# A transformer block on one core: projections and transposes placed anew over the even steps, the second layer norm moved up, the bias sum behind the rounding

## What is computed

```python
x = x + attn(layernorm(x))          # x: 16 x 512 x 256
x = x + ffn(layernorm(x))
# attn: qkv = x @ qkv_w.T + qkv_b; softmax(q k^T / 4) v; then @ proj_w.T + proj_b
# ffn:  clip(x / input_scale, -448, 448) rounded to float8_e4m3fn, times input_scale;
#       then @ (weight_fp8 * weight_scale) + bias
```

## Time and profile before

| | |
|---|---|
| median of three runs | 1002.81 us |
| the profiled execution | 1001.61 us |
| its span, first to last instruction | 999.2 us |
| mean granted clock of TensorE | 0.976 |
| TensorE busy | 929.2 us, 93% |
| VectorE busy | 847.7 us, 85% |
| ScalarE busy | 657.6 us, 66% |
| GpSimd busy | 523.8 us, 52% |

### The profile page before, as it was taken

One profiled execution on the slowest core, in us unless ns is written; L12 is line 12 of the kernel. 1 busy time (PEld: TensorE's weight loads), 2 busy tenths in 40 slices (PEclk: granted clock), 3 DMA queues, 4 the chain that ended last, 5 costly groups with the idle time before them and its releaser, 6 DMA issues.

```text
span 999.2 us, 16767 instructions
## 1 busy us (share of the span) xinstructions
PE 929.2 (93%) x5828; PEld 444.6 (44%) x5828; DVE 847.7 (85%) x1250; ACT 657.6 (66%) x1209; POOL 523.8 (52%) x533
## 2 busy tenths in 40 slices
PE   4799999999999999999999999999999999998974
PEld 3453344444444454444444444444444444433323
DVE  3688889898989899898989989898998989889735
ACT  2147777666767767766777766766776766666750
POOL 3332437557382846647384764738385563715162
PEclk9779999999999999999999999999999999999995
DMA  4972635436254555625355653625555362541010
GB/s 149 135 110 39 101 52 106 86 73 111 51 103 73 85 86 87 107 55 104 58 96 76 107 87 64 111 48 105 78 91 87 53 112 34 101 47 44 2 43 21
DMA packets 46452, 79.42 MB, mean 79 GB/s; under 512 B 10144, under 2 KB 13344, under 8 KB 46368
## 3 DMA queue, kind: packets, MB, share of 16 engines
q1 hardware_dynamic: 46368, 78.36, 45.9%
HBM read 18.42 MB, written 8.39 MB: 27 GB/s over the span
## 4 chain that ended last, share of the span: by engine, by line
PE 59%; POOL 25%; DVE 6%; issue 5%; ACT 2%; DMA 1%; SPq 1%; POOLq 0%; DVEq 0%; ACTq 0%
PE ps_t L471 18%; PE ps_o L505 16%; PE ps_s L487 6%; POOL parts L974 5%; PE ps_m L421 5%; PE ps_m L397 5%; PE ps_m L385 3%; POOL hq L1016 3%; POOL hn L1012 3%; POOL h L1006 3%; POOL hn L996 3%; POOL parts L972 2%; PE ps_m L453 2%; DVE mx L717 2%; POOL oT_p L958 2%
## 5 line engine op out<-in xcount | busy, mean ns | idle before, releaser
L595 ACT ACTIVATE pt<-ps_t 128x512 f32<-128x512 f32 x1024 | 558.0, 598 | 222.3 <-PE ps_t L471 218.9
L717 DVE TENSOR_REDUCE mx<-ps_s 128x2 f32<-128x1024 f32 x512 | 613.2, 1209 | 46.8 <-PE ps_s L487 43.6
L471 PE MATMUL ps_t<-qs,ks 50*128 50x512 f32 x1024 | 394.4, 454 | 11.2 <-ACT pt L595 11.0
L487 PE MATMUL ps_s<-ks,qs 48*128 48x512 f32 x1024 | 374.8, 459 | 4.5 <-DVE mx L717 2.7
L471 PEld LDWEIGHTS ps_t<-qs,ks 50*128 50x128 f32 x1024 | 164.8, 185 | 295.9 <-ACT pt L595 203.1
L505 PE MATMUL ps_o<-pt,vt 128*32 128x512 f32 x2048 | 272.5, 604 | 0.0
L983 POOL TENSOR_TENSOR on<-ot,rden 128x256 f32<-128x256 f32 x63 | 39.1, 621 | 241.1 <-DVE rden L778 241.1
L487 PEld LDWEIGHTS ps_s<-ks,qs 48*128 48x128 f32 x1024 | 155.5, 186 | 15.8 <-issue 7.5
L385 PE MATMUL ps_m<-xnT_p,wqkv_p 128*128 128x512 f32 x360 | 104.8, 420 | 1.0 <-POOL xnT_p L952 1.0
L974 POOL TENSOR_TENSOR parts<-parts 128x512 f32<-128x512 f32 x60 | 80.8, 1347 | 4.9
L505 PEld LDWEIGHTS ps_o<-pt,vt 128*32 128x32 f32 x2048 | 40.4, 108 | 86.5 <-issue 86.0
(11 more groups left out here) (94 smaller groups left out, 798.5 us busy)
## 6 DMA issues: line engine op xcount, KB each, us to landing
qs<-parts SPq DMA_DIRECT2D x192, 128.0 KB, 4.5
ks<-parts SPq DMA_DIRECT2D x192, 128.0 KB, 5.3
xin<-in_x SPq DMA_DIRECT2D x16, 512.0 KB, 3.6
xres<-in_x SPq DMA_DIRECT2D x16, 512.0 KB, 4.3
out<-h SPq DMA_DIRECT2D x32, 256.0 KB, 2.0
qs<-nmax SPq DMA_DIRECT2D x256, 4.0 KB
pt<-in_qkv_wT SPq DMA_DIRECT2D x1, 768.0 KB, 5.7
pt<-in_proj_wT SPq DMA_DIRECT2D x1, 256.0 KB, 5.7
```

The lines of the kernel that those rows point to most:

```text
L471: nc.tensor.matmul(ps_t[:, g, :], ks[par][rows, slot, keys], qs[par][rows, slot, :], start=True, stop=True).then_inc(st_done, 1)
L487: done = nc.tensor.matmul(ps_s[:, s % 2, g, :], qs[par][rows, slot, queries], ks[par][rows, slot, :], start=True, stop=True)
L595: nc.scalar.activation(pt[n % 2][:, w % 2 + 2 * a, w // 2, :], ps_t[:, a, :], ACT.Exp, scale=SCALE).then_inc(exp_done, 1)
L717: dve.tensor_reduce(mx[:, r, :, s % QUARTER], ps_s[:, s % 2, :, :], AX_X, ALU.max).then_inc(max_done, 1)
```

## The change

The table of steps is changed in five places, each as it says. The first Q/K product is cut into two bursts at steps 2 and 4 (slots 0 and 1 keep it whole at step 4, since steps 0 and 2 transpose x there); the general form with part and parts replaces the special case of the last block. V's second half and the first transpose of x change places (24 and 22). The output product of the second half of the tokens stands whole in step 0, instead of in steps 0 and 2, and with it its residual sum. LN2's last two statistics come at steps 1 and 2, its end at 3, power_of_two at 6, rounding_constant at 7. In GpSimd's order layernorm_h stands ahead of the first split, and add_linear_bias directly behind round_fp8. Behind L383 all line numbers are one lower than before (L800 is L799 now).

```diff
-PROJECT_QK = (4, 6, 8, 10)
-PROJECT_QK_REST = 12
+PROJECT_QK = ((2, 4), (6,), (8,), (10, 12))
+PROJECT_QK_1 = ((4,), (6,), (8,), (10, 12))
 TRANSPOSE_HQ = 14
 LINEAR = (16, 18)
-PROJECT_V = (20, 22)
-TRANSPOSE_X = (24, 26)
+PROJECT_V = (20, 24)
+TRANSPOSE_X = (22, 26)
 TRANSPOSE_X1 = (0, 2)
-PROJECT_OUT = ((28, 30), (0, 2))
+PROJECT_OUT = ((28, 30), (0, 0))
...
-LN2_SUM = (31, 31, 3, 4)
-LN2_END = 5
-POWER_OF_TWO = 8
-ROUNDING_CONSTANT = 9
+LN2_SUM = (31, 31, 1, 2)
+LN2_END = 3
+POWER_OF_TWO = 6
+ROUNDING_CONSTANT = 7
...
-                for m, (pw, px, c) in enumerate(products):
+                for m in range(6 * part // parts, 6 * (part + 1) // parts):
+                    pw, px, c = products[m]
...
                 if present(2):
                     out_divide(u - 2, 1)
-                if present(0) and u > 0:
-                    split(u, 0)
                 if present(3):
                     layernorm_h(u - 3)
                 if present(0) and u > 0:
+                    split(u, 0)
                     split(u, 1)
                 if present(3):
                     round_fp8(u - 3)
+                    add_linear_bias(u - 3)
                 if present(0) and u > 0:
                     split(u, 2)
                 if present(2):
@@
                 if present(2):
                     low_oT(u - 2, 0)
-                if present(3):
-                    add_linear_bias(u - 3)
                 if present(-1):
                     layernorm_x(u + 1, 1 - par)
```

More of the change, by code:

```diff
@@ L368, in transpose_x, with project_qk @@
                 last.then_inc(xt_done, 1)
-            def project_qk(u, n, rest=False):
+            def project_qk(u, n, part, parts):
                 start = u == 0
                 bank = ps_s[:, n // 2, n % 2, :] if start else ps_m[:]
-                if not start and not rest:
+                if not start and part == 0:
                     take_bank("project_qk", n, u)
-                if n == 0:
+                if n == 0 and part == 0:
                     pe.wait_ge(xnT_low, 2 * u + 2)
@@ L381, in project_qk @@
                 products = [(pw, px, c) for pw, px in PAIRS for c in range(NC)]
-                if n == 3:
-                    products = products[3:] if rest else products[:3]
-                for m, (pw, px, c) in enumerate(products):
+                for m in range(6 * part // parts, 6 * (part + 1) // parts):
+                    pw, px, c = products[m]
                     last = nc.tensor.matmul(bank, wqkv_p[:, pw, c, first:first + P], xnT_p[:, px, c, :],
-                                            start=(m == 0 and not rest), stop=(m == 2 and rest) or m == 5)
-                if n < 3 or rest:
+                                            start=m == 0, stop=m == 5)
+                if part == parts - 1:
                     last.then_inc(qk_done, 1)
@@ L525, in slot @@
                         transpose_max(u - 1, TRANSPOSE_MAX.index(s))
-                    if s in PROJECT_OUT[1] and present(3):
-                        project_out(u - 3, 1, PROJECT_OUT[1].index(s))
+                    for j in range(2):
+                        if s == PROJECT_OUT[1][j] and present(3):
+                            project_out(u - 3, 1, j)
                     if u == 0 and s in TRANSPOSE_X1:
@@ L531, in slot @@
                         transpose_x(1, TRANSPOSE_X1.index(s))
-                    if s in PROJECT_QK and present(0):
-                        project_qk(u, PROJECT_QK.index(s))
-                    if s == PROJECT_QK_REST and present(0):
-                        project_qk(u, 3, rest=True)
-                        if u == 0:
+                    if present(0):
+                        for n, steps in enumerate(PROJECT_QK if u > 1 else PROJECT_QK_1):
+                            if s in steps:
+                                project_qk(u, n, steps.index(s), len(steps))
+                        if u == 0 and s == PROJECT_QK_1[3][-1]:
                             bias()
@@ L649, in slot @@
                         copy_xnT(u, TRANSPOSE_X1.index(s))
-                    if s in PROJECT_QK[:3] and present(0):
-                        copy_qk(u, par, PROJECT_QK.index(s))
-                    if s == PROJECT_QK_REST and present(0):
-                        copy_qk(u, par, 3)
+                    for n in range(2 * NT):
+                        if s == PROJECT_QK[n][-1] and present(0):
+                            copy_qk(u, par, n)
                     if s == TRANSPOSE_HQ and present(3):
```

## The result

| | before | after |
|---|---|---|
| median of the runs | 1002.59 us (1002.17 to 1005.25) | 1060.72 us (1051.06 to 1067.17) |
| profiled execution, its span | 1001.61, 999.2 us | 1051.06, 1048.9 us |
| mean granted clock of it | 0.976 | 0.934 |

The ratio after to before, over fast runs, is 1.050, with a 95% interval of 1.0435 to 1.0564; the medians of the table, which take in one run of after that counts as slow (1067.17 us), lie 58 us apart. So the change is slower, as forecast, but by 50 to 58 us instead of 22, and outside the range. Both kernels issue 16767 instructions. (A line number of the middle of the kernel is one lower in after than before: L404 is the L405 of the earlier trace rows, L799 the L800 of the earlier trace rows.)

What follows compares the result with a forecast made beforehand. TensorE, with its in-order queue, was taken to set the end. The profiled 1001.6 us plus 9.5 for net waits and 13 for the clock gave 1024, and the median's 1.2 more gave 1025 us; whole range 1004 to 1042.

Steps and rivals of the forecast that it cites:

- The walk through both engines: VectorE and GpSimd followed through a middle slot to step 8, giving a TensorE wait of 2.6 us there.
- The clip's end: GpSimd's clip in the second layer norm, which power_of_two waits for, was to end 14.7 us into the slot.
- VectorE's wait: At power_of_two, for GpSimd's clip: some 2.3 us, with the reduction of step 7 queued behind.
- TensorE's at 2.6: At step 8's transpose of maxima, TensorE was to wait 2.6 us for VectorE's reduction of step 7.
- The step-18 wait: Linear layer's second half waiting for finish_linear; the earlier bias sum was to remove it, gaining 1.3 us a slot.
- step 1: Second product of scores waits for the maximum's split; one output burst in step 0 was to gain 0.2 us.
- the clip is in time: Rival: GpSimd's clip causes no wait at step 8, so the gains stand and the time is 975 us; chance 0.1.
- Net in slots 3 to 15: 2.6 - 2.1 = +0.5: Step 8's new wait of 2.6 us less gains of 2.1 us a slot; times 13, +7 us.
- the exchange of V and x: Half of V at step 24 in place of transposes of x, covering the split: 0.6 us a slot gained.
- Slot 16: I estimate +3: Slot with the layer norm but no projections, so TensorE reaches step 8 earlier: 3 us lost.
- 1.24 in three slots of four: Clock falls behind step 8's wait, slowing the Q/K burst by 1.24 us in three of four of 14 slots: +13 us.
- The median of the runs is 1.2 us above the profiled one: Step from the profiled execution's forecast, 1024 us, to the median of the runs, 1025 us.

Runs made afterwards that it cites:

- due89: Changed kernel with power_of_two back at step 8 and rounding_constant at step 9; 986.70 us, 0.977 of the kernel before.
- due78: Changed kernel with power_of_two at step 7 and rounding_constant at step 8; 986.19 us, 0.982 of the kernel before.
- due69: Changed kernel with rounding_constant alone back at step 9, power_of_two still at 6; 1027.05 us, 1.015 of the kernel before.
- quiet_pool: Changed kernel with GpSimd's round_fp8 directly behind layernorm_h and both splits behind it; 1108.38 us, 1.102 of the kernel before.
- bias_late: due69 with add_linear_bias back in its old place behind low_oT; 1044.25 us, 1.039 of the kernel before.
- pad_late1: due69 with one more unused product at step 20, behind the wait; 1047.96 us, 1.038 of the kernel before.
- warm_drain: due89 with three unused products at each even step from 2 to 12 of slot 17; 977.37 us, 0.971 of the kernel before.
- filler: Changed kernel with nine unused products ahead of step 8's transpose of maxima in 14 slots; 1029.13 us, 1.019 of the kernel before.

## Why the prediction was right in kind and wrong in size

**Right.** The walk through both engines. The clip's end was forecast at 14.7 in the slot and came at 14.6; VectorE's wait at 2.3, and was 2.2; TensorE's at 2.6, and was 2.46, in 13 slots, and 2.96 in slot 16. The step-18 wait went (3.15 to 1.80 us, forecast 1.3), step 1 gained 0.20 as forecast. due89 and due78 show that the early place of the two VectorE operations is the whole loss, and that without it the change wins. Their ratios of 0.977 and 0.982, set on 1002.6 us, are 979 and 984, not far from the 975 of the rival "the clip is in time": its price was nearly right, its condition was not met.

**Wrong, step by step.** The step that failed is the net of +0.5 us a slot: its walk moved rounding_constant to step 7 and put it at nothing, where it cost a second wait of 0.83 us. Two more terms, slot 16 and the clock, were of the right kind and too small.
- "Net in slots 3 to 15: 2.6 - 2.1 = +0.5". It was +1.57: 2.52 at step 8, 0.83 at step 9, less gains of 1.8 instead of 2.1. The larger part is an operation that the prediction moved without costing it: rounding_constant, now at step 7, stands ahead of the split of the maximum. It met GpSimd's splits there and took 1.6 us instead of 0.68, and step 9 grew by 0.83 (due69 takes this away alone; quiet_pool shows that the length does it). The prediction had seen the like effect on power_of_two (0.92 against 0.69) and did not ask it of the other. The rest is the exchange of V and x, 0.25 instead of 0.6. Together, over 13 slots, 13.4 us too little.
- "Slot 16: I estimate +3". It was +9.8. The wait there is 2.96 us, no burst of projections follows it, and the clock stayed low for 20.5 us. 6.8 us too little. I had no walk for this slot, only an estimate.
- "1.24 in three slots of four". The number of slots was near (9 of 13), the price was not: 18.5 us in 9 slots is 2.1 each, since the low clock lasts 3.4 to 17 us, past the burst and over whole steps. 5.5 us too little. The text had both ends, 1.2 and "with some steps of scores behind, up to 2.5", and took the lower one.
- "The median of the runs is 1.2 us above the profiled one". With a clock that falls in some slots and not in others, executions differ: 1051 to 1067. The median is 9.7 above the profiled one.
- With 1.7 us for slot 2, the start and the end these make the 36 us between 1025 and 1060.7. All erred in one direction, which is why the range, built from single terms, did not reach.

On the clock, the rule in the Trainium skill ("TensorE: Matmul & The Clock Gate", section "Why this matters for your kernels"), no gap longer than about 3 us, would have kept it up. In after, bias_late and pad_late1 it fell behind gaps of 2.46 us, in due69 it did not, in quiet_pool it was low at the end of gaps of 2.06, and in slot 17 of due89 it was low with gaps of 0.75 between sparse steps. The forecast was right to weigh it against the rows.

## What to carry to other kernels

When an operation is moved up in an in-order queue, find when its input is ready and which reduction or split stands behind it that another engine needs: here two steps earlier cost 3.3 us a slot, one step earlier nothing. Cost each moved operation anew beside its new neighbours, and look at the parts apart: the one call that mattered (the bias sum) gave 1.3 of the 1.8 us a slot that the change gains without the early place.

Where TensorE has little to do between its waits, unused products can be worth more than they cost (warm_drain); in a single wait of 2.5 us they may be (filler). Without them the time can change by 2% with 0.2 us of work a slot (due69 against pad_late1, 1027 and 1048 us), so do not read such a shift as the effect of the edit alone.

## What the runs showed that was not expected

- The same wait of 2.46 us on TensorE is followed by a low clock in 0, 2, 7, 9, 11 or 13 of 13 slots, in kernels whose slots differ by 1.0 us at most without a fall, and on different chips; 0 and 2 are the same kernel, as are 9 (after) and 11. One of 2.06 comes with a low clock in all 13 (quiet_pool), one of 3.41 also; the old ones of 1.28 in none. A low stretch of the changed kernel's middle slots lasted 3.4 us at the least and 17 in one slot. The kernel with one more product of 0.2 us a slot took 20 us more in all (pad_late1, on another chip).
- Kernels with added work were faster: 18 products in warm_drain, on one chip; 126 in filler, against the changed kernel on other chips.
- A VectorE operation of 0.68 us took 1.62 when it started 0.22 us behind GpSimd's subtraction of two fp32 tensors; when it started 0.1 us ahead it took 0.67, and the subtraction 1.72 instead of 1.29. And power_of_two 1.03 instead of 0.69 (quiet_pool, where GpSimd waits meanwhile).
